# One step of maxima moved behind the first scores, two additions of the exponentials' sums moved to TensorE, and the loop over the batches written out

## The reference, cut to what matters

```
q = layernorm(x) @ Wq * scale;   k, v = split(media @ Wkv)
sim  = where(mask, q k^T, -max)                # per head: 256 x 1601
attn = softmax(sim);  out = attn @ v           # per head: 256 x 64
x = x + tanh(attn_gate) * (out @ Wo)
```

## Time and profile before

| what | value |
|---|---|
| median of 3 runs | 960.75 us (960.44, 960.75, 965.2) |
| the profiled execution's own time | 964.57 us |
| its span, first to last instruction | 962.8 us |
| mean granted TensorE clock, share of full | 0.965 |
| PE busy | 867.5 us (90%) |
| DVE, ACT, POOL busy | 589.8, 442.3, 478.9 us |

### The profile page before, as it was taken

The page is one execution under the profiler, slowest core; times in us unless marked ns, Lnnn a source line. Parts: engine busy times, 40 slices in busy tenths (PEclk is TensorE's granted clock), DMA queues, the critical chain, the costliest instruction groups (busy, mean ns, idle before and its releaser), DMA issues.

```text
span 962.8 us, 19827 instructions
## 1 busy us (share of the span) xinstructions
PE 867.5 (90%) x7811; PEld 721.4 (75%) x7811; DVE 589.8 (61%) x877; ACT 442.3 (46%) x663; POOL 478.9 (50%) x243
## 2 busy tenths in 40 slices
PE   2689999999999999999999999999997789976996
PEld 2587778788878877788778788888776568756884
DVE  5665678868558787774779868556755131533143
ACT  2264555555345565454545655446543332513241
POOL 0047666667736777665666767746776500000000
PEclk9699999999999999999999999999999789997998
DMA  8000001000000100000000000000024000003000
GB/s 264 14 1 2 1 2 35 2 2 1 2 3 1 33 4 1 1 1 2 2 1 1 1 1 1 1 2 1 2 66 124 1 1 0 1 2 88 0 0 22
DMA packets 19633, 16.69 MB, mean 17 GB/s; under 512 B 850, under 2 KB 18659, under 8 KB 19427
## 3 DMA queue, kind: packets, MB, share of 16 engines
q1 hardware_dynamic: 19554, 15.51, 5.3%
HBM read 14.46 MB, written 1.05 MB: 16 GB/s over the span
## 4 chain that ended last, share of the span: by engine, by line
PE 69%; POOL 12%; DVE 7%; issue 5%; ACT 4%; DMA 1%; SPq 1%; POOLq 0%; DVEq 0%; ACTq 0%
PE psum L914 18%; PE psum L315 13%; PE psum L928 13%; POOL acc L409 8%; PE psum L885 5%; PE psum L951 3%; PE psum L851 3%; PE psum L984 3%; PE psum L993 3%; PE psum L1039 2%; ACT od L487 2%; PE psum L944 2%; POOL acc L404 2%; DVE mx L675 2%; POOL acc L416 1%
## 5 line engine op out<-in xcount | busy, mean ns | idle before, releaser
L675 DVE TENSOR_REDUCE mx<-psum 128x2 f32<-128x800 f32 (+2 forms) x256 | 249.8, 991 | 125.8 <-PE psum L885 112.8
L409 POOL TENSOR_TENSOR acc<-acc,ring 128x1024 f32<-128x1024 f32 x128 | 306.4, 2394 | 17.3
L493 ACT ACTIVATE ring<-psum 128x1024 f32<-128x1024 f32 x192 | 197.0, 1027 | 87.6 <-PE psum L914 79.1
L404 POOL TENSOR_TENSOR acc<-ring 128x1024 f32<-128x1024 f32 x32 | 76.6, 2393 | 260.3 <-ACT ring L493 260.3
L928 PE MATMUL psum<-ring,v 128*64 128x256 f32 (+1 forms) x1664 | 186.7, 381 | 1.7
L928 PEld LDWEIGHTS psum<-ring,v 128*64 128x64 f32 (+1 forms) x1664 | 116.8, 137 | 60.6 <-DVE k_lo L668 3.9
L914 PE MATMUL psum<-nm,maskrow 64*128 64x256 f32 (+1 forms) x832 | 132.3, 306 | 1.8 <-DVE maskrow L657 1.4
L914 PE MATMUL psum<-q_hi,k_hi 64*128 64x256 f32 (+1 forms) x832 | 122.8, 284 | 0.0
L914 PE MATMUL psum<-q_lo,k_hi 64*128 64x256 f32 (+1 forms) x832 | 122.0, 282 | 0.0
L914 PE MATMUL psum<-q_hi,k_lo 64*128 64x256 f32 (+1 forms) x832 | 122.0, 282 | 0.0
L885 PE MATMUL psum<-k_hi,q_hi 64*128 64x400 f32 (+1 forms) x512 | 98.1, 376 | 20.3 <-ACT od L487 12.0
(11 more groups left out here) (149 smaller groups left out, 1425.4 us busy)
## 6 DMA issues: line engine op xcount, KB each, us to landing
nat<-in_ctx_dram SPq DMA_DIRECT2D x8, 768.0 KB
w<-in_L_xattn_W_dram SPq DMA_DIRECT2D x2, 1024.0 KB, 7.6
xs<-in_x_dram SPq DMA_DIRECT2D x4, 256.0 KB, 5.4
ring<-in_L_xattn_Wkv_dram SPq DMA_DIRECT2D x1, 1024.0 KB, 6.5
wq<-in_L_xattn_Wq_dram SPq DMA_DIRECT2D x1, 1024.0 KB, 8.6
wo<-in_L_xattn_Wo_dram SPq DMA_DIRECT2D x1, 1024.0 KB, 9.8
out_dram<-t_res SPq DMA_DIRECT2D x4, 256.0 KB, 2.2
mask<-in_mask_BxS_bk_dram SPq DMA_DIRECT2D x4, 200.1 KB, 6.0
```

Of the source, the lines that this page charges most:

```text
L404: nc.gpsimd.tensor_tensor(acc[:, :, :, :], ring[:, 0, :, :, :], ring[:, 1, :, :, :], ALU.add)\
L409: nc.gpsimd.tensor_tensor(acc[:, :, :, :], acc[:, :, :, :], ring[:, g, :, :, :], ALU.add)\
L493: nc.scalar.activation(ring[:, g, :, :, :], score_set[m % 2].rearrange("p (h i q) -> p h i q", h=2, i=2), ACT.Exp).then_inc(S["p_ready"], 1)
L675: nc.vector.tensor_reduce(mx[:, t, :, c], aux_pair[BANK[item] // 2][:, :, 0:min(c1, KEYS) - c0], axis=AX.X, op=ALU.max).then_inc(S["m_max" ...
```

## The change

Three edits, in the kernel's own terms:

1. `row_phase` puts step 1 of M behind group 0 of S. The steps before and after, and the banks, keep their places.
2. POOL no longer does the fold (line 412) and the tail (line 416). Item D on PE becomes six matmuls in one accumulation per head: two on the tail's 65 rows of `ring`, ahead of the wait for POOL, then for both halves of `acc` two each. `acc_done` counts five steps per pair instead of seven.
3. The loops over batches on SP, ACT, DVE, PE and POOL are written out as straight code; all their waits compare with constants.

```diff
 def row_phase(j):
-    out = [("M", j + 1, 0)]
-    for g in range(KEY_GROUPS):
+    out = [("M", j + 1, 0), ("S", j, 0), ("M", j + 1, 1)]
+    for g in range(1, KEY_GROUPS):
         out += [("M", j + 1, g + 1), ("S", j, g)]
     return out
...
-               "acc_done": GROUPS * PAIRS, "rstd_ready": 1}
+               "acc_done": (GROUPS - 2) * PAIRS, "rstd_ready": 1}
...
-            with sp.Fori(0, BATCH - 1) as b:
+            for b in range(BATCH - 1):
                 upto(sp, "t_full", b, TUNITS)
...
                     for g in range(2, GROUPS - 1):
                         upto(pool, "p_ready", b, n0 + g + 1)
-                        upto(pool, "acc_done", b, n0 + g - 1)
+                        upto(pool, "acc_done", b, a0 + g - 1)
                         nc.gpsimd.tensor_tensor(acc[:, :, :, :], acc[:, :, :, :], ring[:, g, :, :, :], ALU.add)\
                             .then_inc(S["acc_done"], 1)
-                    upto(pool, "acc_done", b, n0 + GROUPS - 2)
-                    nc.gpsimd.tensor_tensor(acc[:, :, 0, :], acc[:, :, 0, :], acc[:, :, 1, :], ALU.add)\
-                        .then_inc(S["acc_done"], 1)
-                    upto(pool, "p_ready", b, n0 + GROUPS)
-                    upto(pool, "acc_done", b, n0 + GROUPS - 1)
-                    nc.gpsimd.tensor_tensor(acc[0:TAIL, :, 0, :], acc[0:TAIL, :, 0, :],
-                                            ring[0:TAIL, GROUPS - 1, :, 0, :], ALU.add).then_inc(S["acc_done"], 1)
...
-            with pool.Fori(1, BATCH - 1) as b:
+            for b in range(1, BATCH - 1):
                 sums(b, True)
...
-            with act.Fori(0, BATCH - 1) as b:
+            for b in range(BATCH - 1):
                 attention(b, BODY)
...
-                        upto(pe, "acc_done", b, (n + 1) * GROUPS)
                         bank = aux[BANK[("A", n)]]
                         for h in range(2):
-                            last = mm(bank[h * HD:(h + 1) * HD, TOK:2 * TOK], ones[:, 0:HD],
-                                      acc[:, h, 0, :], start=True, stop=True)
+                            mm(bank[h * HD:(h + 1) * HD, TOK:2 * TOK], ones[0:TAIL, 0:HD],
+                               ring[0:TAIL, GROUPS - 1, h, 0, :], start=True, stop=False)
+                        upto(pe, "acc_done", b, (n + 1) * (GROUPS - 2))
+                        for i in range(2):
+                            for h in range(2):
+                                last = mm(bank[h * HD:(h + 1) * HD, TOK:2 * TOK], ones[:, 0:HD],
+                                          acc[:, h, i, :], start=False, stop=(i == 1))
                         last.then_inc(S["ad_full"], 1)
```

More of the change, by code:

```diff
@@ L282, in upto @@
         def upto(eng, name, b, k):
[L284 to L287, removed]
+            if b * PER[name] + k > 0:
                 eng.wait_ge(S[name], b * PER[name] + k)
@@ L397, in sums @@
                 for j in range(PAIRS):
-                    n0 = j * GROUPS
+                    n0, a0 = j * GROUPS, j * (GROUPS - 2)
                     upto(pool, "p_ready", b, n0 + 2)
[L400 to L403, removed]
+                    upto(pool, "ad_full", b, j)
                     nc.gpsimd.tensor_tensor(acc[:, :, :, :], ring[:, 0, :, :, :], ring[:, 1, :, :, :], ALU.add)\
@@ L710, in _ @@
             dve.wait_ge(S["gates_ready"], 1)
-            with dve.Fori(0, BATCH - 1) as b:
+            for b in range(BATCH - 1):
                 attention(b, BODY)
@@ L956, in _ @@
             pe.wait_ge(S["weights_in"], 16 * 3)
-            with pe.Fori(0, BATCH - 1) as b:
+            for b in range(BATCH - 1):
                 attention(b, BODY)
```

## The result

The changed kernel takes 957.56 us (median of 14 runs, 956.46 to 959.25). The kernel before, run beside it, takes 965.24 us (14 runs, 959.71 to 967.78), not the 960.75 of the three runs shown ahead. The ratio is 0.9932 (95% interval 0.9915 to 0.995): faster by 0.7%. Over all 66 executions of this study the kernel before falls into a quicker group (959 to 963 us, mean granted clock mostly 0.969 to 0.971) and a more frequent slower one (963.4 to 967.8 us, 0.962 to 0.966), while the changed kernel's 14 lie together at 0.975 and 0.976. I had forecast 952 us, that is 8.75 less than 960.75; measured are 7.7 less than 965.24, or 6.6 by the ratio. The profiled execution took 958.78 us.

What follows compares the result with a forecast made beforehand. PE, busy 90% of the span, was taken as the bound, its row phase paced by the round trip with ACT; -16.0 + 27.0 - 4.4 - 1.7 - 7.4 - 6.5 = -9.0 us from 960.75 gave 952 us, range 944 to 968.

Steps and rivals of the forecast that it cites:

- The base: Last step of the forecast: the sum of -9.0 us taken from the median 960.75 us, giving 951.8, stated as 952.
- edit 3, with the drop at 184: Batch edges written out save 6.5 us; the clock loss of 1.7 us behind the wait at 182 goes too.
- edit 2, 30 times D less the waits: Four more matmuls in D cost 0.90 us per pair, +27.0 in thirty; five earlier waits for POOL go, -4.4.
- edit 1, 29 pairs: Row phase: S1, PE's end and POOL's start come 0.55 us earlier per pair, 16.0 us saved, bounds 0 and 24.
- last two pairs and behind: Last two pairs, bound by POOL, save 2.9 and 3.3 us, last D and output projection 1.2; together 7.4.
- The first has another order: Remark leaving the first pair out of the 29 pairs counted for edit 1; no size given.
- clock 1.00 from 60 us: Expected sign in the changed profile: granted clock 1.00 from 60 us to the last D.
- `negl` at 0.23 everywhere: Expected sign on DVE: every write of `negl` takes 0.23 us; above 2 us would be wrong.
- The row phase doesn't follow: Rival, chance 0.12: in the row phase the `od` wait becomes one at M2 or M3; 16 us missing, 968 us.
- Writing out brings nothing: Rival, chance 0.10: holes at the batch edges are something else or straight code has its own; 958.5 us.
- GpSimd's port: Rival, chance 0.10: `negl` on DVE blocked by POOL's additions, PE waits some 1.1 us per pair, +33, 985 us.
- More gain: Rival, chance 0.08: the row phase's beat follows S0 and saves 0.83 us per pair; 944 us.

Runs made afterwards that it cites:

- edit 3 alone: The kernel before with only the batch loops of all five engines written out: 956.0 us, ratio 0.9921.
- edits 2 and 3: The changed kernel with step 1 of M back ahead of group 0 of S: 966.2 us, ratio 1.0022 to the kernel before.
- the version of 945.0 us: The changed kernel with the fold back on POOL except in the last two pairs of the last batch, tail still on PE: 945.0 us, ratio 0.9807.
- edit 1 alone: The kernel before with only step 1 of M moved behind group 0 of S: 955.3 us, ratio 0.9913.
- edit 2 alone: The kernel before with only fold and tail moved from POOL to PE, row order and loops as before: 984.1 us, ratio 1.0188.
- both (10): The changed kernel with the batch loops kept as before, so edits 1 and 2 together: 965.4 us, ratio 1.0018 to the kernel before.
- edits 1 and 3: The changed kernel with fold and tail back on POOL: 951.1 us, ratio 0.9872 to the kernel before.

## Why the prediction was right or wrong

Two steps failed: the time that the sum was taken from, and the first pair, which had no term. Inside the sum edit 1 was sized too large, and edit 2, sized too costly, made up for most of it.

**The base.** The last step of the sum was wrong. I took -9.0 from the median of three runs, 960.75, and called the profiled 964.57 unusual. The kernel before lies between 959.1 and 967.8, more than half of its executions at 964.4 to 966.8, and its median is 965.2 here (962.6 to 965.2 in the later comparisons): the profiled execution was the ordinary one. I had written myself that the quick runs may lack a clock loss that the terms take away, and then took the whole 9.0 from them. From 964.57 my own sum gave 955.6, against 958.8 profiled. Choosing 952 instead made a gain of 9.0 into one of 13.2 against the measured base, where 6.6 to 7.7 were measured.

**The terms**, from the traces of before, edit 3 alone, edits 2 and 3, and all three:

| part of the program | predicted | measured |
|---|---|---|
| up to the first D | 0 | +2.7 |
| edit 3, with the drop at 184 | -8.2 | -9.0 |
| edit 2, 30 times D less the waits | +22.6 | +18.5 |
| edit 1, 29 pairs | -16.0 | -10.8 |
| last two pairs and behind | -7.4 | -7.2 |
| sum | -9.0 | -5.8 |

From the first D on, -8.5 was measured for -9.0. That is close by luck: edit 1 fell short by 5.2, and edit 2 cost 4.1 less than I had priced.

**The first pair.** "The first has another order" was all I said of it, and no term or bound stood for it. It cost 2.7 in the profiled execution: 0.6 was there already when its M0 started, and the pair took 24.3 instead of 22.3. The low clock lasted to 62 instead of to 58, and `negl` was held for 1.84 at 67.3; without the hold the version of 945.0 us gained 0.7 in this pair. Tying the length of the low clock to the order was tested once and not borne out. What sets it stays open. My signs "clock 1.00 from 60 us" and "`negl` at 0.23 everywhere" failed here and nowhere else ahead of the last D.

**Edit 1.** The mechanism was right: M2 waits for the reduction (1.57 behind M0, 1.6 predicted), and POOL moves by 0.57. The size was off. S0 comes 0.29 behind M0 instead of 0.18, which the earlier trace rows had already (303.27 to 303.55 from M step 1 to S0), so S1 moved by 0.49 instead of 0.55. Of this the pairs kept 0.3 to 0.5, the first pair of each batch nothing. Beside edit 3 alone, with POOL still doing all its additions, the order is worth 6.0 in the 31 pairs and not 11.2.

**Edit 2.** D itself grew by 0.87 (0.90 predicted). But I had counted POOL only where the waits view lists a wait for it. The additions were the bound in the pair with W as well, which lost 0.7, so edit 2 brought 7.6 back in those 29 pairs and not 4.4. The last two pairs took 17.7 and 16.8, from D's end to D's end, against my 17.5 and 16.8.

**Edit 3, 6.5 predicted, and 1.7 for the drop at 184.** Pairs 1 to 31 lost 8.4 us from the kernel before to edit 3 alone, of which some 1.5 is that drop. The holes I priced (1.42 and 1.33 over an ordinary one) left 0.69 behind, so the jump proper is 1.2 and 1.1. What I did not see is what edit 3 does beside edit 2: POOL's third addition starts 0.08 behind the second's end in the loop and 0.14 in straight code, and with edits 2 and 3 together none is late. In the kernel before the loop has 0.14 too, and `negl` was late only in the two pairs of the jumps.

**Behind the last D** the output projection went from 9.32 to 8.65, 0.7 less as predicted, and all from D's end on from 198.6 to 197.8.

**The rivals.** *The row phase doesn't follow*: fell, S1 and POOL's start moved, and edit 1 alone took 955.3. *Writing out brings nothing*: fell (956.0). *GpSimd's port*: in the changed kernel only in the first pair, but real. I gave it a decision point of 0.1 us; the free `negl` of the changed kernel come 0.03 to 0.06 ahead of the third addition's start, and 0.08 more was enough. My price, 33 us for all pairs, met 35. It struck edit 1 alone (5 pairs), edit 2 alone (11), both (10) and edits 1 and 3 (3). The rule of the Trainium skill (SBUF — State Buffer, Who interferes with whom) that the later of the two blocks for a whole instruction agrees with these traces: 2.4 us against 0.23 on DVE, and ACT, which that page says never waits, at 0.31 in all 32. *More gain*: no.

## What to carry to other kernels

Price work by the engine that bounds, per unit: taking 2.7 us from POOL paid only where POOL was the bound, 6.8 us in the last two pairs together and up to 0.7 in each pair with W, and cost PE some 0.8 in each of the other 25. Move only as much as the other engine can't hide, and only in the units where it can't. Before summing against a median of three, look at how far the runs lie apart, and at which disturbances the profiled one holds.

## What was not expected of the hardware

A VectorE instruction of 0.23 us that comes just when GpSimd begins its next addition stands on an edge. Up to 0.003 us behind that start it still took 0.23, from 0.007 on it was held until the addition's end, for 2.4 us on DVE and up to 3.8 us in PE's pair (25.04 against 21.27). From the second addition's end to the third's start it is 0.14 us in straight code and in the middle batches of the kernel before, but 0.08 in the loop of the kernels with edit 2, and there that decided in 11 pairs. What makes it 0.08 no run shows.
